# Decoder layer on one core: scan state turned by VectorE blocks and a DRAM scratch, feed-forward tiles over the score banks, a halved ln_g pass

## The reference

```
x = layernorm(x + attention(x))         # 16 heads of 32, q, k, v, o with a low-rank part
x = layernorm(x + x * state)            # state_t = decay * state_(t-1) + ctx_t * ctx_t
x = layernorm(x + ffn(x))
# ffn: h = layernorm(gelu(silu(q8(rms(x)) @ ternary(w1).T + b1))) * ln_g + ln_b
#      y = q8(rms(h)) @ ternary(w2).T + b2     q8: rows scaled to 127 and rounded
```

## Time and profile before

| what | value |
|---|---|
| runs | 1042.36 us median of 3 (1042.34 to 1043.55) |
| profiled execution | 1039.61 us, of which the span from first to last instruction is 1037.8 us |
| busy | PE 941.8 us (91%), DVE 859.1 (83%), ACT 826.3 (80%), POOL 548.5 (53%) |
| mean granted TensorE clock | 0.966 |
| chain that ended last | DVE 33%, PE 25%, ACT 17%, issue 13%, POOL 7%, DMA 3% |

### The profile page before, as it was taken

How to read it: one execution, slowest core, us unless ns; L and a number is a source line. 1 busy time by engine, 2 the same in 40 slices (tenths; PEclk the granted TensorE clock), 3 DMA queues, 4 the chain that set the end, 5 groups by cost and what they waited for, 6 DMA issues and landing times.

```text
span 1037.8 us, 23337 instructions
## 1 busy us (share of the span) xinstructions
PE 941.8 (91%) x9244; PEld 647.8 (62%) x9260; DVE 859.1 (83%) x1490; ACT 826.3 (80%) x957; POOL 548.5 (53%) x767
## 2 busy tenths in 40 slices
PE   5998987999999999999999999999999999977515
PEld 3766756676777667676767767676767777654102
DVE  4578868889797989889897979898897979897766
ACT  3646686888989798888888897988889897977684
POOL 2332338274654639373755647383746546472643
PEclk9999998999999999999999999999999999999768
DMA  9432200313132222323141212323131412122213
GB/s 361 158 113 113 73 3 21 75 49 88 22 85 52 55 62 56 81 53 85 27 110 22 75 46 61 71 53 85 52 85 22 97 40 75 22 63 54 53 34 89
DMA packets 106351, 73.67 MB, mean 71 GB/s; under 512 B 91385, under 2 KB 91385, under 8 KB 104450
## 3 DMA queue, kind: packets, MB, share of 16 engines
q1 hardware_dynamic: 105522, 70.34, 25.3%
q10 hardware_dynamic: 720, 1.84, 0.5%
HBM read 41.73 MB, written 8.40 MB: 48 GB/s over the span
## 4 chain that ended last, share of the span: by engine, by line
DVE 33%; PE 25%; ACT 17%; issue 13%; POOL 7%; DMA 3%; SPq 1%; DVEq 0%; ACTq 0%; POOLq 0%
PE bank L1484 8%; PE bank L1345 7%; DVE neg_max L965 6%; POOL h L549 5%; DVE stats L1022 3%; ACT h L727 3%; DVE h L1096 3%; ACT junk L737 3%; ACT h L742 3%; DVE fz L1101 2%; DVE qk_parts L988 2%; PE bank L1485 2%; ACT L727 2%; DVE rows L1038 2%; DVE qx L1063 2%
## 5 line engine op out<-in xcount | busy, mean ns | idle before, releaser
L965 DVE TENSOR_REDUCE neg_max<-wave 128x8 f32<-128x2048 f32 x64 | 146.2, 2284 | 29.4 <-PE wave L1370 29.4
L549 POOL TENSOR_TENSOR h<-h,g_tile 128x2048 f32<-128x2048 f32 x30 | 139.2, 4640 | 39.1 <-ACT h L742 39.1
L659 ACT ACTIVATE probs<-wave 128x1024 f32<-128x1024 f32 x128 | 124.2, 1023 | 28.2 <-PE wave L1394 27.9
L1484 PE MATMUL bank<-w,xqT 128*128 128x512 fp8e4 x496 | 130.0, 385 | 17.5 <-DMA xqT<-xq 13.6
L439 POOL TENSOR_SCALAR attn_hi<-attn 128x256 fp32r<-128x256 f32 x64 | 28.3, 442 | 174.3 <-DVE attn L1004 159.4
L697 ACT ACTIVATE rows<-rows,rstd 128x512 f32<-128x512 f32 x96 | 74.4, 807 | 41.9 <-POOL rstd L455 23.7
L1096 DVE TENSOR_TENSOR h<-h,b_tile 128x2048 f32<-128x2048 f32 x32 | 84.1, 2629 | 18.6 <-POOL h L549 18.0
L721 ACT ACTIVATE h<-bank,qx 128x512 f32<-128x512 f32 x124 | 82.3, 689 | 20.0 <-PE bank L1485 16.7
L1491 PE MATMUL bank<-w,hqT 128*128 128x512 fp8e4 x416 | 94.3, 380 | 0.3 <-DMA hqT<-h 0.3
L1484 PEld LDWEIGHTS bank<-w,xqT 128*128 128x128 bf16 x496 | 46.7, 99 | 74.9 <-DMA xqT<-xq 9.9
L1345 PE MATMUL bank<-xT_hi,wq_hi 128*128 128x256 f32 x256 | 78.8, 308 | 0.1
(11 more groups left out here) (184 smaller groups left out, 2736.9 us busy)
## 6 DMA issues: line engine op xcount, KB each, us to landing
ctx_sb<-ctxT SPq DMA_DIRECT2D x16, 512.0 KB, 3.7
rows<-x SPq DMA_DIRECT2D x16, 512.0 KB, 4.0
out<-rows SPq DMA_DIRECT2D x32, 256.0 KB, 2.1
xT_in<-xT SPq DMA_DIRECT2D x15, 512.0 KB, 4.0
h<-w1T SPq DMA_DIRECT2D x4, 1024.0 KB, 14.0
h<-w2T SPq DMA_DIRECT2D x4, 1024.0 KB, 5.0
h<-Wq SPq DMA_DIRECT2D x1, 1024.0 KB, 5.9
h<-Wk SPq DMA_DIRECT2D x1, 1024.0 KB, 9.4
```

What stands on the lines that cost most here:

```text
L549: po.tensor_tensor(h_of(b, q)[:, :], h_of(b, q)[:, :], g_tile[:, :], ALU.mult).then_inc(done, 1)
L659: ac.activation(probs[:, kt, :, :], wave[:, :, kt * T:(kt + 1) * T], ACT.Exp, scale=SM_SCALE).then_inc(S["probs_ready"], 1)
L965: dv.tensor_reduce(neg_max[:, :, :], wave[:, :, :].rearrange("p j (t k) -> p j t k", t=NT), axis=AX_X, op=ALU.max, negate=True).then_inc(S ...
L1484: pe.matmul(p[:, :], xqT[:, q, kc, :], w1[:, kc, n * FW:(n + 1) * FW], start=(kc == 0), stop=False)
```

## The change

- The state: after the clamp DVE turns the 32x32 blocks of the state in two instructions (each 128x512) into `state_blocks`, which is the buffer `x_round`; SP writes it to a DRAM scratch (512 KB), waits for that, and reads it back in four transfers of 128 KB, each into 32 partitions of `ctx_sb` (`move_state`, issued as the second thing of SP's next step). `layernorm2_sum` reads `ctx_sb` and not PSUM. PE's `r` is gone. The host lays out ctx and decay to fit. `load_ctx` waits for the two sums of `layernorm2_sum`.
- `add_halves` is gone; PE sums the keys of group 0 as those of the others. `quantise_x` no longer waits for PE's `weighted`.
- `f` tiles go to banks 6, 7, 4, 6, 1, 2, 3, 7. PE's `shifted(j, 0)` moves behind `y(j, 0)` and waits for silu 6 of that step's feed-forward.
- POOL: `inverse_std3(j-3, 1)` goes ahead; `g_mul(j-2, 1)` is cut into two halves of 128x1024: the first waits for the statistics of the second norm and stands ahead of `inverse_std2`, the second waits for `maxima(j, 3)` and stands behind `x_rms`. `res2` waits for DVE's last `quantise_z` where it waited for `scan`.
- DVE: `quantise_z(j-2, 0)` goes ahead of `z_add(j-2, 1)`, and `scan(j)` ahead of `quantise_z(j-2, 1)`.
- ACT: `z_square(j-2, 1)` goes from ahead of `zq_store(j-2, 0)` to between ACT's `shiftT(j+1, 0)` and silu 4.

```diff
-        bank_no.update({("f", u): (6, 7, 4)[u % 3] for u in range(8)})
+        bank_no.update({("f", u): (6, 7, 4, 6, 1, 2, 3, 7)[u] for u in range(8)})
...
             def load_ctx(b):
-                wait(sp, "rT_ready", b - 1, 2)
+                wait(sp, "ln2", b - 1, 4)
...
+            def move_state(b):
+                wait(sp, "scan_done", b, 7)
+                wait(sp, "state_moved", b - 1, 16 * SB)
+                sp.dma_start(state_scratch.rearrange("a i s x -> (a i) (s x)"),
+                             state_blocks).then_inc(S["state_out"], 16)
+                wait(sp, "state_out", b, 16)
+                for s in range(SB):
+                    to = state_rows[s * HD:(s + 1) * HD, :].rearrange("p (a x) -> p a x", a=SB)
+                    sp.dma_start(to, state_scratch[:, :, s, :].rearrange("a i x -> i a x")
+                                 ).then_inc(S["state_moved"], 16)
...
             # SP body and drain
                 if alive(j, -1):
                     load_xT(j + 1)
+                move_state(j - 1)
...
             # POOL body
-                    wait(po, "scan_done", j - 1, 5)
+                    if alive(j, 3):
+                        wait(po, "z_quant", j - 3, 12)
+                    else:
+                        wait(po, "scan_done", j - 1, 7)
                     res2(j - 2)
...
-                if alive(j, 2):
-                    g_mul(j - 2, 1)
+                if alive(j, 3):
+                    inverse_std3(j - 3, 1)
+                if alive(j, 2):
+                    wait(po, "ln2", j - 1, 6)
+                    g_mul_half(j - 2, 0)
                 if alive(j, 1):
                     inverse_std2(j - 1)
                     x_rms(j - 1)
-                if alive(j, 3):
-                    inverse_std3(j - 3, 1)
+                if alive(j, 2):
+                    wait(po, "shift_split", j, 8)
+                    g_mul_half(j - 2, 1)
...
             # ACT body
                 if alive(j, 2):
-                    z_square(j - 2, 1)
                     zq_store(j - 2, 0)
...
                     qk_hi(j + 1, 1)
                     shiftT(j + 1, 0)
+                if alive(j, 2):
+                    z_square(j - 2, 1)
                 if alive(j, 1):
                     silu(j - 1, 1)
...
             # DVE scan
+                for q in range(NT):
+                    dv.transpose(blocks[:, q, :, :, :],
+                                 ctx_sb[:, :, q * P:(q + 1) * P].rearrange("p k (s c) -> p k s c", c=HD)
+                                 ).then_inc(S["scan_done"], 1)
...
             # DVE body (add_halves also goes from lead and body)
                 if alive(j, 2):
+                    quantise_z(j - 2, 0)
                     z_add(j - 2, 1)
-                    quantise_z(j - 2, 0)
...
+                if alive(j, 0):
+                    scan(j)
                 if alive(j, 2):
                     quantise_z(j - 2, 1)
-                if alive(j, 0):
-                    scan(j)
...
             # PE body (r(j, 0) and r(j, 1) go)
                     y(j, 0)
+                shifted(j, 0)
...
-                if alive(j, -1):
-                    shifted(j + 1, 0)
```

More of the change, by code:

```diff
@@ L386, in drain @@
             def drain():
+                move_state(LAST)
                 transpose_z(THIRD, 1)
@@ L549, in g_mul, with g_mul_half @@
                 po.tensor_tensor(h_of(b, q)[:, :], h_of(b, q)[:, :], g_tile[:, :], ALU.mult).then_inc(done, 1)
+            def g_mul_half(b, i):
+                wait(po, "h_normed", b, 2)
+                if b == 0:
+                    po.wait_ge(u_gain, 16 * 2)
+                cols = slice(i * INNER // 2, (i + 1) * INNER // 2)
+                half = h_of(b, 1)[:, cols]
+                po.tensor_tensor(half, half, g_tile[:, cols], ALU.mult).then_inc(S["g_mul"], 1)
             def z_rms(b, q):
@@ L1016, in scan @@
                                  ALU.max).then_inc(S["scan_done"], 1)
+                wait(dv, "scan_done", b, KC + 1)
+                wait(dv, "xq_stored", b - 1, 1)
+                blocks = state_blocks.rearrange("p (s q k c) -> p q k s c", s=SB, q=NT, c=HD)
+                for q in range(NT):
+                    dv.transpose(blocks[:, q, :, :, :],
+                                 ctx_sb[:, :, q * P:(q + 1) * P].rearrange("p k (s c) -> p k s c", c=HD)
+                                 ).then_inc(S["scan_done"], 1)
             def statistics(ln, b, q, k, tile_rows):
@@ L1034, in layernorm2_sum @@
             def layernorm2_sum(b, q):
-                wait(dv, "rT_ready", b, q + 1)
+                wait(dv, "state_moved", b, 16 * SB)
                 wait(dv, "norm1", b, q + 1)
-                dv.scalar_tensor_tensor(rows_of(b)[:, q, :], bank_of("r", q, b), SCAN_SCALE, rows_of(b)[:, q, :],
-                                        ALU.add, ALU.mult).then_inc(S["ln2"], 1)
+                state = state_rows.rearrange("p (a q x) -> p q a x", a=SB, q=NT)[:, q, :, :]
+                x_rows = rows_of(b)[:, q, :].rearrange("p (a x) -> p a x", a=SB)
+                dv.scalar_tensor_tensor(x_rows, state, SCAN_SCALE, x_rows, ALU.add, ALU.mult).then_inc(S["ln2"], 1)
                 statistics(2, b, q, 3 * q + 1, rows_of(b)[:, q, :])
@@ L1088, in z_add @@
                 if b < PRIOR:
-                    wait(dv, "g_mul", b, q + 1)
+                    wait(dv, "g_mul", b, 1 if q == 0 else 3)
                 elif q == 0:
@@ L1232, in body @@
                 if alive(j, 0):
-                    add_halves(j)
                     maxima(j, 1)
@@ L1385, in shifted @@
                 wait(pe, "shiftT_stored", b, c + 1)
+                if c == 0:
+                    wait(pe, "silu_done", b - 2, 7)
                 parts = qk_parts[c % 2]
@@ L1402, in weighted @@
                 if c == 0 and b >= 2:
-                    wait(pe, "silu_done", b - 2, 6)
+                    wait(pe, "silu_done", b - 2, 3)
                 wait(pe, "probs_ready", b, 2 * (c + 1))
@@ L1409, in weighted @@
                                   start=(kt == 0), stop=(kt == NT - 1))
-                if c == 0:
-                    wait(pe, "half_added", b, 1)
-                    for i in range(GH):
-                        last = pe.matmul(bank[4][i * HD:(i + 1) * HD, T:2 * T], ones[:, :], half_sum[:, i, :],
-                                         start=True, stop=True)
-                for kt in range(NT if c > 0 else 0):
+                for kt in range(NT):
                     for i in range(GH):
@@ L1464, in o_second_half @@
                 split_product(bank_of("o", q, j - 1)[:, :], o_terms(q, (2, 3)), first=False).then_inc(S["o_ready"], 1)
-            def r(j, q):
-                r_product(take(j, "r", q, "scan_done", j - 1, 5), q)
-            def r_product(p, q):
-                for kc in range(KC):
-                    last = pe.transpose(p[:, kc * P:(kc + 1) * P], ctx_sb[:, kc, q * P:(q + 1) * P], ident[:, :])
-                last.then_inc(S["rT_ready"], 1)
             def f(j, u):
@@ L1523, in drain @@
                 wait(pe, "probs_ready", LAST, 8)
-                wait(pe, "scan_done", LAST, 5)
-                for q in range(NT):
-                    r_product(bank_of("r", q, LAST), q)
                 drain_y(THIRD, 0)
@@ L1605, in lead @@
                 shiftT(1, 0)
-                shifted(1, 0)
             def body(j):
```

46 lines of the change are left out of this document (19 added, 27 removed).

## The result

| | before | after |
|---|---|---|
| median of runs | 1042.35 us (1039.85 to 1043.55, 4 runs) | 1054.61 us (1053.25 to 1056.03, 4 runs) |
| ratio of after to before | | 1.0116, 95% interval 1.0094 to 1.0137 |
| span of the profiled execution | 1037.8 us | 1051.4 us |

What follows compares the result with a forecast made beforehand. The prediction took a four-engine ring of waits to bind, with a second ring 0.33 us a period short of it. 13 x 0.42 = +5.5, +0.5, -0.9 and -0.5 gave +4.6 us, so 1047.0; range 1036 to 1055.

Steps and rivals of the forecast that it cites:

- rival 4: POOL's second half pass or later `res1` holds `quantise_x` or the scan: up to +0.5 a period, 1053.5; chance 0.12.
- The moved square: ACT's `z_square(1)` between f start and the gelus: silu 7 ends 10.53 after f start, +0.42 a period.
- second ring: Waits from PE's f start over silus, gelus, POOL, `shift_rows` of group 2, `shifted(j, 2)` to next f start; slack 0.33 a period.
- Rival 1: Silus 4 to 7 keep PE's pace behind `z_square`, giving back 0.33 a period: 1036.7; chance 0.14.
- No table load: At ACT's moved Square between silus: no table switch counted, against some 69 us by the skill's list.
- PE's lost work: Eight transposes and their stall gone, key sums added, ahead of `shifted(j, 2)`: PE only waits about 1.3 longer; value 0.
- DVE's transposes: Two of 128x512 at the step's end, 0.88 each, +1.8 together, in DVE's idle time; value 0.
- ACT's `normalise(2)` and PE's `shifted(j, 3)` have that slack: POOL's first half pass starts `inverse_std2` some 0.35 us later; these two readers were said to absorb it.
- xqT: POOL's second half pass can hold `quantise_x` on the way to this transfer: +0.5 for all such periods together.
- First step: Removed transposes lie on PE's path there too; against the added key sums: -0.5.
- Drain: Removed transposes stand on the chain between the o products and `y`: 0.87 of their 1.03 goes, -0.9.
- Rival 3: The longer hole at `shifted(j, 2)` lowers PE's clock behind it: 13 x 1.7 = +22 on top, 1069; chance 0.07.

Runs made afterwards that it cites:

- e7: Changed kernel without the state's way and POOL's half passes; moved square, DVE order, tile banks and `shifted(j, 0)` place stay: 1046.9 us, ratio 1.0040.
- e6: Changed kernel with only the state's way undone (PE turns the state into PSUM, `add_halves` back), half passes kept: 1047.9 us, ratio 1.0053.
- e5: Kernel before with only POOL's ln_g pass for half 1 in two half passes, `inverse_std3(1)` ahead of them: 1050.9 us, ratio 1.0073.
- e10: Kernel before with the state's way alone (DVE blocks, DRAM scratch, sums over both probs tiles), POOL's order untouched: 1108.3 us, ratio 1.063.
- e4: Changed kernel with eight unread PE transposes of the identity between `shiftT(j, 2)` and `shifted(j, 2)`: 1054.9 us, ratio 1.0117.
- e1: Changed kernel with POOL's ln_g pass for half 1 whole again ahead of `inverse_std2`, `inverse_std3(1)` behind `x_rms`: 1105.6 us, ratio 1.062.
- e13: Changed kernel with POOL's `attn_split(j, 1)` behind `inverse_std3(1)` instead of ahead of it: 1052.0 us, ratio 1.0102.
- e2: Changed kernel with both half passes behind `inverse_std2` and `x_rms`, without the two waits in front of them: 1120.1 us, ratio 1.074.
- e12: Changed kernel with POOL's `inverse_std3(1)` between `inverse_std2` and `x_rms` instead of ahead of the first half pass: 1064.0 us, ratio 1.020.
- e11: Changed kernel without state's way and half passes, `z_square(1)` between `zq_store(0)` and silu 0, other f banks, f3 behind row maxima: 1037.9 us, ratio 0.9961.
- e9: Changed kernel without state's way and half passes, `z_square(1)` between `zq_store(0)` and silu 0, other f banks, `shiftT` ahead of f3: 1043.4 us, ratio 1.0006.
- e14: Changed kernel, state's way kept, with e11's square place, f banks and f3 wait, and e13's POOL order: 1054.0 us, ratio 1.012.

## Why the prediction was wrong

Direction and first mechanism were right; the size was not. The measured 1054.6 still lies in the stated range of 1036 to 1055, but by luck: that edge was drawn for rival 4, and something else brought the time there. By the ratios above, with before at 1042.4: the moved square and what goes with it +4.2 (e7), the half passes +1.3 more (e6), the state's way +6.6 more (after). The 1.3 is smaller than its interval; periods and f starts show the parts sharper. These prices hold in this order only: on the kernel before, the half passes alone cost +7.6 (e5) and the state's way alone +66 (e10).

- **The moved square** (+0.42 a period forecast): about +0.25, from 57.4 to 57.64 in e7. `shift_rows` of group 2 ends 0.3 later than before. The chain of the second ring was right, and PE's wait in front of f3 is gone as forecast. The size was for silu 7 at 10.53; it ends at 10.43, against 10.1 in most periods before (9.74 to 10.5), so the delay is 0.3. Rival 1 (ACT isn't late) is out.
- **No table load**: right. Each of the 16 profiled kernels has 47 table loads, wherever its Square stands. The Trainium skill, ScalarE: Activation LUTs, "Table sets: the hidden batching unit", doesn't list Square among what every set holds; these runs show no switch for it.
- **PE's lost work is worth 0 in the loop**: right (1.22 idle, e4).
- **DVE's transposes**: 1.31 for both, not 1.8, in idle time of the loop. **The state's transfers**: 2.6 us out and 2.8 in (median from issue to landing), hidden by far. Right, but beside the point.
- **The step that failed: the reader of the state.** I costed how the state gets to SBUF and left the instruction that reads it at its old 0.68. With two SBUF operands it stands still until a POOL operation that was there first is over: 0.38 in each period in the kernel after, beside the 0.74 of `attn_lo`, and 3.5 with POOL's old order (e1, e10). I had a row for such a hold, 4.70 for 1.28, and used it for other instructions only. The Trainium skill, SBUF — State Buffer, "SBUF: two separate sides", says of the pair of ports that DVE and GpSimd share that whoever starts first keeps it for the whole instruction, and that DVE wants it with two SBUF inputs. e1 (4.21 beside 5.12) and e6 (0.68 with one operand in PSUM) agree.
- **"ACT's `normalise(2)` and PE's `shifted(j, 3)` have that slack"**: right for the half pass alone (e6: 57.66), wrong once the 0.38 came on top: `inverse_std2` starts 44.0 after f start instead of 42.8, `shift_rows` of group 3 ends at 48.14 instead of 46.9, PE waits, 58.02. That is +0.36 in 13 periods, 4.7 us. The 0.38 reaches PE at two places. DVE's row maxima of group 3 and their split are late as well, so `shiftT(j, 3)` starts 8.76 after `shifted(j, 2)`, in e6 8.44; `shifted(j, 3)` starts 10.65 after it, in e6 10.16. e13 takes away the first wait (8.48) and only part of the second (10.46), which is why it brings only half.
- **xqT** (+0.5 forecast): `xq` is stored at 53.1 after f start, 0.9 later than before, while f start moved by 0.6. Four periods of the kernel after are 0.5 to 1.7 longer than 58.02, 3.6 us together. Before, a long period was made good in the next (57.92, then 56.97); after, it isn't (59.69, then 58.03). The term was seven times too small. The last section has what these four have in common.
- **First step** (-0.5 forecast): +1.9, all of it with the state's way (128.8 in e6 and e7, 130.8 after). PE has no slack there: the row maxima come 0.5 later from the third on, 0.9 by the seventh, beside the added key sums and DVE's transposes, and 1.9 by the eighth. In between the clock is lower for longer. PE in windows of 4 us (length, busy, granted clock, DMA), after, then before:

```profile
104.00:108.00 4.00, 0.94 (x4) 0.89 0.00 0
108.00:112.00 4.00, 3.71 (x40) 0.50 0.11 13
112.00:116.00 4.00, 4.00 (x46) 0.76 0.31 118
```

```profile
104.00:108.00 4.00, 2.06 (x20) 0.89 0.00 0
108.00:112.00 4.00, 4.00 (x48) 0.68 0.40 131
112.00:116.00 4.00, 4.00 (x67) 1.00 0.02 4
```

  The difference in clock is worth 4 x 0.18 + 4 x 0.24 = 1.7 us at full rate. e4 kept PE busy there with transposes and got 0.50 and 0.84, so what sets it stays open; that it comes with the state's way is shown (e6 has 0.71 and 1.00 there).

- **Drain** (-0.9 forecast): -1.3, though not only from the chain. The last f of the loop waited 3.56 us for xqT before and ran its next 5 us at a mean clock of 0.72; after, it waited 1.61 and ran at 1.00.

Rival 3 (the clock) didn't come: behind the holes of 1.2 to 1.4 us at `shifted(j, 2)` the granted clock stays at 1.00 in the twelve periods from the second f start on. Its mechanism exists in this kernel behind longer holes: 0.50 behind the 3.9 us of e2, and in half of the periods behind the 3.6 us of e1.

Rival 4 named POOL's passes and, at 1053.5, comes nearest. It had them hold `quantise_x` and the scan; what they hold on the path is the sum of the second norm.

## What to carry to other kernels

Moving an operand from PSUM to SBUF changes the instruction that reads it, not only the one that made it: check what POOL runs beside it, even where both are well under a microsecond. A long POOL pass has a few windows in a period in which DVE runs what no pass held here: reductions, and instructions with an operand in PSUM. One large operand alone is no safe sign, since the `tensor_scalar` of the earlier trace rows has no more and stood still until a pass was over. Moved by 0.7 us out of its window (e12), a half pass cost some 9 us. And a wait that grows on PE can cost clock on top (e1, e2). Work that must be done on an engine in the ring costs least where that engine already waits for the bottleneck's first tile (e11), not between its later tiles.

## What the hardware showed that I had not expected

**Transposing transfers with an instruction fetch beside them land later.** Two stretches of the kernel after, from an issue of xqT to f start, issues with their us to landing, the first with fetches (queues q8 and q14), the second without:

```profile
q8 instruction: 1, 0.02, 1.0%
q14 instruction: 1, 0.01, 0.3%
...
xqT<-xq SPq DMA_TRANSPOSE x1, 5.8
```

```profile
xqT<-xq SPq DMA_TRANSPOSE x1, 3.4
```

Over the 16 profiled kernels, the 145 xqT transfers with no fetch in the 3.4 us behind their issue landed in 3.3 to 3.5 us, the 111 with one in 3.4 to 6.0. Which steps are hit moves with the program: with PE's 8 extra instructions of e4 other periods are long. Every transfer over 3.5 us had one. No run forced a fetch onto a transfer, so this is a correlation. The longest took 2.6 us more than the usual 3.4, so a kernel with less than that to spare can pay in some periods; here the slack at f start fell from about 1.5 to 0.8.

**The clock near the start differs between profiles.** In 5 of the 16 profiled executions (e2, e9, e11, e13, e14) the second row maxima start at 42.2 to 43.1 us instead of near 40. PE of e11 and of before, windows of 4 us:

```profile
28.00:32.00 4.00, 2.17 (x17) 0.77 0.73 288
32.00:36.00 4.00, 4.00 (x26) 0.50 0.66 225
36.00:40.00 4.00, 4.00 (x24) 0.88 0.20 51
```

```profile
28.00:32.00 4.00, 3.61 (x34) 0.92 0.67 260
32.00:36.00 4.00, 4.00 (x40) 1.00 0.67 236
36.00:40.00 4.00, 4.00 (x50) 1.00 0.17 40
```

The changed kernel's own runs have spans of 1051.4 twice and 1054.2 twice. That this is the same shift isn't shown, since only one of them has a profile. Whether e11's order or chance put its profile among the five isn't settled either; its runs spread from 1035.3 to 1041.9. It is why the terms above are read from periods and not from single times.
